# A delay table in a list schedule, causal scores in three fills instead of four, and the set-up moved into the scheduled stream

## What is computed

```python
x = x + local_attention(layernorm(x))          # 7 neighbours of each token, biases
x = x + cross_attention(layernorm(x), context) # 120 keys, biases
x = x + ffn_block(layernorm(x))                # adds inside:
#   h = h + causal_attention(rmsnorm(h, n1)); h = h + moe(rmsnorm(h, n2))
#   moe: gate of 8, softmax, top 2, silu(h @ up.T) @ down.T, inner width 1024
```

## Time and profile before

| | us |
|---|---|
| median of 3 runs (lowest, highest) | 4187.93 (4185.14, 4190.39) |
| time of the profiled execution | 4194.42 |
| its span, first to last instruction | 4192.7 |
| PE busy | 3875.9 (92%) |
| DVE, POOL, ACT busy | 2506.0, 2490.8, 1857.2 |
| PE's mean granted clock | 0.976 |

### The profile page before, as it was taken

The page is one execution under the profiler, slowest core; times in us unless marked ns, Lnnn a source line. Parts: engine busy times, 40 slices in busy tenths (PEclk is TensorE's granted clock), DMA queues, the critical chain, the costliest instruction groups (busy, mean ns, idle before and its releaser), DMA issues.

```text
span 4192.7 us, 96887 instructions
## 1 busy us (share of the span) xinstructions
PE 3875.9 (92%) x40328; PEld 3152.4 (75%) x40328; DVE 2506.0 (60%) x4820; ACT 1857.2 (44%) x3393; POOL 2490.8 (59%) x3156
## 2 busy tenths in 40 slices
PE   4799999999999999999999999999999999999997
PEld 3577777777777777777777777777777777777775
DVE  4666665565665665665665665665665665665642
ACT  1344444444444444444444444444444444444442
POOL 4766665665665665666655666655656656656621
PEclk9799999999999999999999999999999999999998
DMA  4101111111111111111111111111111111111100
GB/s 142 61 36 61 47 50 64 44 54 63 41 55 64 39 58 64 39 58 64 39 58 64 39 58 64 39 58 62 41 58 64 37 59 53 46 62 49 48 7 8
DMA packets 87142, 221.54 MB, mean 53 GB/s; under 512 B 8316, under 2 KB 53688, under 8 KB 70328
## 3 DMA queue, kind: packets, MB, share of 16 engines
q1 hardware_dynamic: 86712, 215.34, 14.5%
HBM read 164.92 MB, written 50.39 MB: 51 GB/s over the span
## 4 chain that ended last, share of the span: by engine, by line
PE 77%; ACT 9%; POOL 6%; DVE 4%; DMA 2%; issue 2%; SPq 0%; POOLq 0%; DVEq 0%
PE ps L822 10%; PE ps L813 10%; PE ps L794 8%; PE ps L693 8%; PE ps L658 7%; PE ps L674 7%; PE ps L758 7%; PE ps L728 7%; ACT prob L902 6%; PE ps L680 4%; POOL chunks L1016 3%; PE ps L771 2%; PE ps L640 2%; ACT held L879 2%; DMA k_windows<-passed_k 1%
## 5 line engine op out<-in xcount | busy, mean ns | idle before, releaser
L1021 POOL TENSOR_TENSOR chunks<-v_windows,xT 128x560 f32<-128x560 f32 (+1 forms) x384 | 869.0, 2288 | 424.7 <-DVE xT L1114 422.1
L1016 POOL TENSOR_TENSOR chunks<-rest,k_windows 128x512 f32<-128x512 f32 (+1 forms) x384 | 549.4, 1452 | 519.2 <-DMA k_windows<-passed_k 463.2
L902 ACT ACTIVATE prob<-ps 120x1024 f32<-120x1024 f32 (+1 forms) x512 | 620.0, 1240 | 436.7 <-PE ps L736 436.7
L1137 DVE TENSOR_REDUCE nmax_pair<-ps 128x16 f32<-128x1920 f32 (+2 forms) x320 | 712.9, 2228 | 126.2 <-PE ps L703 108.0
L1032 POOL TENSOR_SCALAR_AFFINE_SELECT prob<-prob 128x512 f32<-128x512 f32 x512 | 313.4, 636 | 383.4 <-ACT prob L902 383.4
L813 PE MATMUL ps<-xT,w_up 128*128 128x256 f32 x2048 | 481.1, 383 | 12.2 <-ACT xT L863 11.6
L1094 DVE TENSOR_REDUCE xT<-chunks 128x32 f32<-128x512 f32 (+1 forms) x384 | 296.0, 772 | 311.2 <-POOL chunks L1016 311.1
L758 PE MATMUL ps<-prob,va 120*32 120x256 f32 (+2 forms) x6144 | 337.7, 371 | 143.0 <-ACT prob L902 139.5
L822 PE MATMUL ps<-w_down,held 128*128 128x256 f32 x2048 | 455.1, 380 | 4.2 <-DVE held L1183 4.2
L1094 DVE TENSOR_REDUCE held<-chunks 128x80 f32<-128x560 f32 (+1 forms) x384 | 296.2, 771 | 271.0 <-POOL chunks L1021 269.2
L728 PE MATMUL ps<-held 32*120 32x256 f32 (+2 forms) x6144 | 389.2, 367 | 51.6 <-ACT prob L902 45.7
(11 more groups left out here) (147 smaller groups left out, 6724.8 us busy)
## 6 DMA issues: line engine op xcount, KB each, us to landing
k_windows<-passed_k SPq DMA_DIRECT2D x64, 1024.0 KB, 4.9
v_windows<-passed_v SPq DMA_DIRECT2D x64, 1024.0 KB, 7.0
x<-in_x SPq DMA_DIRECT2D x64, 256.0 KB, 2.9
passed_k<-rest SPq DMA_DIRECT2D x64, 256.0 KB, 2.0
passed_v<-held SPq DMA_DIRECT2D x64, 256.0 KB, 2.1
out<-x SPq DMA_DIRECT2D x64, 256.0 KB, 2.2
y<-in_ctx SPq DMA_DIRECT2D x64, 120.0 KB, 2.8
w_up<-in_up SPq DMA_DIRECT2D x1, 1024.0 KB
```

The lines of the kernel that those rows point to most:

```text
L902: last = nc.scalar.activation(dst[0:keys], ps[0:keys, first:first + 4, n * T:n * T + dst.shape[2]], ACT.Exp, scale=SCALE)
L1016: last = nc.gpsimd.tensor_tensor(chunk_of(c).rearrange("p (j d) -> p j d", d=D), q_row, window("k", (b + first) * D, (D, n), (1, D)), ALU. ...
L1021: last = nc.gpsimd.tensor_tensor(chunk_of(c).rearrange("p (h i j) -> p h i j", i=HD, j=WINDOW), window("v", b * D + first * HD, (HD, n), ( ...
L1137: nc.vector.tensor_reduce(dst, src, AX_X, ALU.max, negate=True).then_inc(emptied[b], 1)
```

## The change

1. `SENIORITY` goes from 22 to 35, and a table `DELAY` adds a number to the key of some steps: a positive one keeps a step back behind other ready steps, a negative one lets it go ahead.
2. The causal layer's scores take three fills: two with two head groups each, keys 0 to 127 (1,024 columns, like a cross fill), and one with all four head groups, keys 128 to 255 (four times 128 columns in each bank). In every score fill the bfloat16 matmuls of the maximum now come first and the float32 ones last. Fill, exponentials and masks hold the same elements as before; the exponentials of a causal layer are eight instructions in place of four.
3. The set-up block is gone. Its loads are five steps `weights` on SP, in groups, its derivations are steps `derive` on PE, DVE and ACT, all planned with the first sequence's steps; each engine waits once for what it first needs. The reordered weights pass through `prob` instead of `held`, the reordering is done by ACT, and the zeros take two DMAs.

```diff
 def score_units(layer):
-    return [(0, 1), (2, 3)] if layer == CROSS else [(0,), (1,), (2,), (3,)]
+    fills = [((0, 0), (1, 0)), ((2, 0), (3, 0))]
+    return fills if layer == CROSS else fills + [tuple((g, 1) for g in range(4))]
...
-SENIORITY = 22.0
+SENIORITY = 35.0
+DELAY = {("down", None, "PE"): 65, ("project", 2, "PE"): 40, ("scores", 1, "PE"): -10, ("shift", 1, "PE"): -20,
+         ("turn_ctx", None, "PE"): -65, ("turn_out", 0, "PE"): -20, ("untangle", 1, "PE"): 15,
+         ("up", None, "PE"): 55, ("project", 2, "ACT"): 5, ("values", 1, "ACT"): 20, ("gate", None, "DVE"): 25,
+         ("project_out", 0, "DVE"): -35}
+LOADS = (("local_k", "local_v", "local_bk", "local_bv"), ("local_q", "local_o", "local_bq", "local_bo"),
+         ("cross_q", "cross_k", "cross_v", "cross_o", "cross_bv", "cross_bo"),
+         ("causal_q", "causal_k", "causal_v", "causal_o", "cross_bq", "cross_bk", "n1"),
+         ("up", "down", "gate", "n2"))
+def setup_parts():
...
+    loads = [part("weights", (n,), "SP", busy, [], lag=lag)
+             for n, (busy, lag) in enumerate(((2.0, 5.0), (2.0, 6.0), (3.0, 10.0), (4.5, 12.0), (5.5, 18.0)))]
+    part("zeros", (), "SP", 0.6, [], lag=2.5)
+    tables = part("derive", ("tables",), "PE", 1.0, [])
+    part("derive", ("tables",), "DVE", 1.4, [tables])
+    part("derive", ("pick",), "DVE", 0.9, [])
+    part("derive", ("bias",), "DVE", 4.6, [loads[3], ("derive", ("pick",), "DVE")])
+    part("derive", ("scale",), "DVE", 4.3, [loads[3], loads[4]])
+    part("derive", ("cross",), "ACT", 3.6, [loads[2]])
+    part("derive", ("causal",), "ACT", 3.6, [loads[3]])
...
-            for u, gs in enumerate(score_units(layer)):
+            for u, unit in enumerate(score_units(layer)):
                 step = ("scores", (layer, u))
-                a = part(*step, "PE", 1.1 if layer == CROSS else 0.82, [shifted],
-                         [("quad", step)] + [("prob", (layer, g)) for g in gs])
-                a = part(*step, "ACT", 1.9 if layer == CROSS else 1.36, [a], (), [("quad", step)])
+                first = [p for p in held if u == 2]
+                a = part(*step, "PE", 1.04, [shifted] + first[0::2],
+                         [("quad", step)] + [("prob", (layer, g)) for g, kb in unit if kb == 0])
+                held.append(a)
+                a = part(*step, "ACT", 1.9 if u < 2 else 2.3, [a] + first[1::2], (), [("quad", step)])
+                held.append(a)
                 if layer == CAUSAL:
-                    a = part(*step, "POOL", 1.2, [a])
+                    a = part(*step, "POOL", 1.2 if u < 2 else 2.4, [a])
...
+        delay = [DELAY.get((p.name, p.args[0] if p.name in BY_LAYER else None, p.engine), 0.0) for p in parts]
...
-            ready[parts[i].engine].append((SENIORITY * n - left[i], n, i))
+            ready[parts[i].engine].append((SENIORITY * n - left[i] + delay[i], n, i))
...
                     elif name == "scores":
-                        for n, g in enumerate(score_units(L)[u]):
+                        for n, (g, kb) in enumerate(score_units(L)[u]):
+                            key0, keys, q0, qs, col = key_blocks(L, T, C)[kb]
+                            for r in range(4):
+                                rows = slice(32 * r, 32 * r + 32)
+                                nc.tensor.matmul(ps[0:keys, first + r, n * qs:(n + 1) * qs], pick[rows, g, 0:keys],
+                                                 nmaxT[s][rows, q0:q0 + qs], start=(n == 0), stop=False,
+                                                 tile_position=(32 * r, 0), skip_group_check=True)
+                        for n, (g, kb) in enumerate(score_units(L)[u]):
...
-                            for key0, keys, q0, qs, col in key_blocks(L, T, C):
-                                for r in range(4):
-                                    rows = slice(32 * r, 32 * r + 32)
-                                    last = nc.tensor.matmul(ps[0:keys, first + r, n * T + col:n * T + col + qs],
-                                                            pick[rows, g, 0:keys], nmaxT[s][rows, q0:q0 + qs],
-                                                            start=False, stop=True, tile_position=(32 * r, 0),
-                                                            skip_group_check=True)
```

More of the change, by code:

```diff
@@ L77, in sequence_parts @@
 def sequence_parts(T, C):
     out = []
+    weights = [("weights", (n,), "SP") for n in range(len(LOADS))]
+    needs = {("project_rows", "k"): [weights[0]], ("project_rows", "v"): [weights[0]],
+             ("project_rows", "q"): [weights[1]], ("project_out", LOCAL): [weights[1]],
+             ("project_out", CROSS): [weights[2]], ("project_out", CAUSAL): [weights[3]],
+             ("fetch", "k"): [("zeros", (), "SP")], ("fetch", "v"): [("zeros", (), "SP")],
+             ("project", CROSS): [weights[2], ("derive", ("cross",), "ACT"), ("derive", ("bias",), "DVE")],
+             ("project", CAUSAL): [("derive", ("causal",), "ACT"), ("derive", ("scale",), "DVE"),
+                                   ("derive", ("bias",), "DVE")],
+             ("max", CROSS): [("derive", ("tables",), "DVE")], ("max", CAUSAL): [("derive", ("tables",), "DVE")],
+             ("gate", None): [("derive", ("scale",), "DVE")], ("up", 0): [("derive", ("scale",), "DVE")]}
@@ L81, in part @@
+    needs.update({("up", m): needs["up", 0] for m in range(1, 4)})
     def part(name, args, engine, busy, after, takes=(), gives=(), lag=None):
-        out.append(Part(name, args, engine, busy, LAG[engine] if lag is None else lag, tuple(after), tuple(takes),
+        first = engine in ("PE", "SP")
+        also = needs.get((name, args[0] if args else None), []) if first else []
+        out.append(Part(name, args, engine, busy, LAG[engine] if lag is None else lag, (*after, *also), tuple(takes),
@@ L199 @@
 BY_WEIGHT = ("sent", "fetched")
+BY_LAYER = ("moments", "norm", "turn", "project", "max", "round_max", "shift", "scores",
+            "values", "untangle", "turn_out", "project_out")
 class Plan:
     def __init__(self, N, T, C):
-        parts = sequence_parts(T, C)
+        once = setup_parts()
+        parts = once + sequence_parts(T, C)
         at = {p[:3]: i for i, p in enumerate(parts)}
@@ L267, in __init__ @@
                     for j in followers[i]:
[L268 to L271, removed]
+                        for m in range(N) if i < len(once) <= j else (n,):
+                            missing[m, j] -= 1
+                            if not missing[m, j]:
+                                offer(m, j)
+        assert sum(map(len, self.order.values())) == len(todo)
         self.lane = [self.slot["lane", n, ()] for n in range(N)]
@@ L402, in sem @@
             return sems[-1]
+        constants, filled_ones, zeroed = sem("constants"), sem("filled_ones"), sem("zeroed")
+        loaded = [sem(f"loaded{n}") for n in range(len(LOADS))]
+        derived = {what: sem(f"derived_{what}") for what in ("tables", "pick", "bias", "scale", "cross", "causal")}
+        tables_filled = sem("tables_filled")
         filled = [sem(f"filled{b}") for b in range(SINGLES + QUADS)]
@@ L445, in half_max, with once @@
             return nmax_parts[s][:].rearrange("p b (r x) -> p (b r) x", x=32)
+        def once(eng, known, what, signal, count):
+            if what not in known:
+                known.add(what)
+                eng.wait_ge(signal, count)
         def wait_taken(eng, name, n, *args):
```

333 lines of the change are left out of this document (186 added, 147 removed).

## The result

The changed kernel takes 3876.27 us (median of 4 runs, 3873.4 to 3881.16) against 4189.16 for the kernel before beside it: a ratio of 0.9255, with a 95% interval of 0.9238 to 0.9271. The forecast was 3946 with a range of 3895 to 4045.

The account below looks back on a forecast made before the run. PE sets the pace, losing time to waits, low clock and the ends. Waits -153, clock -48, outside the middle -10, fills -4, set-up -27 sum to -242: 3952 profiled, 3946 us as median, range 3895 to 4045.

Parts of the forecast that it names:

- What bounds the kernel, and that the waits go: In the middle 3,500 us PE sets the pace; its 181.3 us of idle time nearly goes, -153 us.
- priced gaps: Work on PE between dependent steps, at cross `values`, causal fills, the maximum and the masks; masks' slack 0.8 us.
- Everything added, I take 0.5 us of waits for a sequence: PE waits left after the reordering, 0.5 us a sequence, bounds 0.2 and 1.8; counted as 28 us in the middle.
- The 0.26 foreseen at the maximum: New PE wait between first and second causal fill: 2.29 us of steps against DVE's 2.55 for the maximum.
- The fills, -4: Causal score fills on PE: three at 4.06 us against four at 4.12, times 64; -4 us, bounds -20 and +6.
- Low-clock spells, -48: PE's low-clock periods behind long waits in the middle go with those waits: -48 us, bounds -20 and -48.
- Rival B: PE's low-clock spells stay, caused by something other than the waits: 3994 us, chance 0.08.
- Outside the middle, -10: A few periods with PE waits and low clock lie outside the middle window: -10 us.
- The set-up, -27: At the start POOL's first k chunk comes 36 us earlier, 9 lost to later sequences' steps: -27, bounds -41 and -15.
- Rival A: POOL's masks come late for causal `values`, the window landing 2.2 us later: +85, 4031 us, chance 0.14.
- D: Slower than before: causal `values` loses 4.0 us a sequence, the last mask 4.8 later than summed; chance 0.03.
- C: More comes in than counted: no waits, start -41, fills -20, giving 3888 us; chance 0.05.

## Why the prediction was right in kind and wrong in size

- **What bounds the kernel, and that the waits go:** right. PE idle in the middle is 0.05% where below 1.5% was named, `values` waits 1.2 us for ACT in the whole span, and stretches are 58.4 where 59.5 was named. Of the priced gaps those at the cross `values`, the causal fills and the masks held, the last with a slack of 0.5 where 0.8 was put; the one at the maximum was short, as foreseen. The order isn't the only thing that does it: by itself it leaves 1.2 us of waits a sequence, fills and set-up without it leave 1.95, and the low clock is gone in either.
- **"Everything added, I take 0.5 us of waits for a sequence":** mis-sized, 0.03 by the profile. The "as much again for what misses by a little" didn't come. The 0.26 foreseen at the maximum came in part: from the first fill's end to the second's start are exactly the 2.55 that were estimated (1949.99 to 1952.54), but the steps between cost 2.45 and not 2.29, so that PE stands only some 0.1, which the profile counts as work. By the profile's idle time this term is 0.47 a sequence too high, 26 us over the 56.
- **The fills, -4:** mis-sized, the largest miss. The third causal fill was put at 1.5, between 1.2 if bound by columns and 1.65 if by instructions; it takes 1.28, close to the columns. bfloat16 first was costed "at nothing" and saves 0.06 a fill, 19 us. Five fills now take 1.19 + 1.19 + 1.28 + 1.22 + 1.23 = 6.11 where six took 4 x 1.03 + 2 x 1.28 = 6.68. PE's work in a stretch fell by 0.69 (59.07 to 58.38), of which 0.57 are the fills, where 0.06 was forecast: 35 us over the 56.
- **Low-clock spells, -48:** right. Rival B is refuted by a clock of 1.00 throughout the middle; the kernel with four more masks brings the spells back by another wait. What the prediction held for B, that the wait alone doesn't decide, is so: in the kernel before 28 of 56 stretches have them. The Trainium skill's rule (TensorE: Matmul & The Clock Gate, What's actually happening) is that the low rate is the default and activity lifts it; both traces are in keeping with it, and neither tells which stretch is hit.
- **Outside the middle, -10:** mis-sized. The last four intervals alone gave 25, and the order alone gives 23 there.
- **The set-up, -27:** first `down` and three intervals gave 23, and the first k chunk is at 31.44 where 29 was estimated; but the reason was wrong. The term let the earlier first chunk carry the start, and kept DVE's 3 us of scaling "within the bound". With the first load behind the set-up the first chunk comes 16 us later and the time is the same (3879.54, where the changed kernel had 3876.27 and 3881.73); in both the first v chunk comes after what POOL and DVE have to do before it. The new set-up doesn't bring the earlier `down` alone either: it stands at 226.87 with the table and at 240.59 without, and at 247.33 with the table and the old set-up.
- **Rival A:** not the case, but near; its wait is confirmed, the low clock that comes with it was not in its price. The shared memory interface (the Trainium skill, GPSIMD Engine Reference, Specifications) changed nothing: a mask takes 638 ns for 636, a chunk 1270 for 1272. **D** needed masks 4.8 us later; 2.7 us more gave 4062.64, still below before.

In the sum: 65 us more in the middle (1.16 a sequence: 0.47 waits, 0.63 work, the rest the clock and rounding between stretches), 15 more at the end, 4 less at the start: the 76 between 3952 and the profiled execution's 3875.6. The range failed since C took no waits and -20 for the fills, and left out the 32 us that the text itself had named as the bound for bfloat16 first. Its lower end, 3895, also stopped short of C: it lies halfway between 3900 and C's 3888 and not, as written, halfway from the forecast.

## What to carry to other kernels

When a fixed order has one wait in each period, look for independent steps to put between producer and consumer and price the gap from the timeline; where all gaps come out positive, take the waits as zero rather than adding a margin, and put the margin into the range. Once the engine that sets the pace doesn't wait, its instructions are all that counts, down to the order of two kinds within a fill. At the start of a program an earlier first transfer is worth only what the chain behind it lets through: hold it back on purpose and see, and look whether the plan has kept the rest of the order.

## What the runs showed of the hardware

Sixteen bfloat16 matmuls of 128 columns take the 0.40 us that eight of 256 take, and the float32 ones 1.11 for 1.03, so that in fills over four row groups the columns count and the number of instructions hardly does. A fill with its bfloat16 matmuls ahead of the float32 ones takes 0.05 to 0.10 us less than the other way round (1.23 for 1.29 in a cross fill, 1.19 for 1.29 in a causal one of two head groups); why, no run here tells.

In the middle of the span PE's granted clock fell behind single waits of 2.2 us and more, for whichever engine, but not behind each: behind one of 2.21 us it was 0.53 for the next 3.40, close to the lower level of 1.2 GHz, behind one of 2.19 it stayed at 1.00. With such a wait in nearly every stretch, 28 of 56 stretches had a mean clock of 0.97 in the kernel before, and 24 of 56 one of 0.97 or less in the kernel with four more masks. Without the table 102 us of idle time in 3,200, in waits of at most 1.7, left the clock at 1.00, and so did the 65 us of the kernel before with the table, in waits of at most 1.0. What decides between two waits of the same length isn't shown.
